# Attention loops of a four-layer model written out tile by tile, with three groups of lead, other load times, and the transposed scores first in each step

## The reference

```python
scores = jnp.einsum('bhqd,bhkd->bhqk', q, k) / np.sqrt(HEAD_DIM)   # 16 heads of 8 channels
attn = jax.nn.softmax(scores, axis=-1)
out = jnp.einsum('bhqk,bhkd->bhqd', attn, v)
```

```python
tp, ti = jax.lax.top_k(probs, TOP_K)          # TOP_K = 2 of NE = 8
def expert_step(acc, params):
    q = (x @ qw.T + qb_)...; k = (x @ kw.T + kb_)...; v = (x @ vw.T + vb_)...
    scores = jnp.einsum('bhqd,bhkd->bhqk', q, k) * scale
    p = jax.nn.softmax(scores, axis=-1)
    o = jnp.einsum('bhqk,bhkd->bhqd', p, v)
    o = o.transpose(0, 2, 1, 3).reshape(B, S, E) @ ow.T + ob_
    return (acc + o * g[..., None], None)
```

## Time and profile before

| | us |
|---|---|
| median of three runs | 4910.73 |
| the runs | 4908.14, 4910.73, 4930.10 |
| the profiled execution, its own time | 4940.64 |
| its span from first to last instruction | 4939.0 |

### The profile page before, as it was taken

The page is one execution under the profiler, slowest core; times in us unless marked ns, Lnnn a source line. Parts: engine busy times, 40 slices in busy tenths (PEclk is TensorE's granted clock), DMA queues, the critical chain, the costliest instruction groups (busy, mean ns, idle before and its releaser), DMA issues. The chain is left out here.

```text
span 4939.0 us, 142944 instructions
## 1 busy us (share of the span) xinstructions
PE 3549.6 (72%) x55309; PEld 2015.0 (41%) x55309; DVE 3202.2 (65%) x3717; ACT 2588.6 (52%) x4898; POOL 700.0 (14%) x1500
## 2 busy tenths in 40 slices
PE   1699999259998965557533288887888887888838
PEld 0355555125556732224422144444444444444414
DVE  2689889338862149984522377777777776777744
ACT  1478888127783432212111167676677666666632
POOL 0000000011000007850300011111111111111120
PEclk6799999669998977778666589898889898888868
DMA  3000000200000012200333444444444444444410
GB/s 53 18 9 8 7 8 8 38 28 13 8 5 18 17 72 86 102 18 4 37 105 109 99 91 94 94 95 89 93 92 98 86 96 87 94 89 94 94 44 21
DMA packets 173983, 286.61 MB, mean 58 GB/s; under 512 B 94796, under 2 KB 139538, under 8 KB 149134
## 3 DMA queue, kind: packets, MB, share of 16 engines
q1 hardware_dynamic: 168670, 272.05, 24.0%
q0 software_dynamic: 4656, 5.18, 0.5%
HBM read 220.57 MB, written 41.52 MB: 53 GB/s over the span
## 5 line engine op out<-in xcount | busy, mean ns | idle before, releaser
L825 ACT ACTIVATE channels_qk<-psum 128x512 f32<-128x512 f32 (+1 forms) x3908 | 2108.7, 592 | 822.6 <-PE psum L693 515.7
L887 DVE TENSOR_REDUCE l2f_chunk_max<-psum 128x2 f32<-128x1024 f32 x1168 | 1386.5, 1223 | 517.1 <-PE psum L666 510.4
L887 DVE TENSOR_REDUCE chunk_max<-psum 128x2 f32<-128x1024 f32 (+2 forms) x848 | 946.6, 1161 | 150.5 <-PE psum L666 110.6
L714 PE MATMUL psum<-channels_qk,l2f_v_and_ones 128*9 128x128 f32 x18448 | 779.7, 292 | 7.0 <-ACT channels_qk L825 5.5
L693 PE MATMUL psum<-l2f_q_parts,l2f_k_parts 51*128 51x128 bf16 x9224 | 495.5, 231 | 245.3 <-ACT channels_qk L825 116.3
L666 PE MATMUL psum<-l2f_k_parts,l2f_q_parts 48*128 48x512 bf16 x2336 | 491.1, 417 | 90.6 <-issue 69.3
L666 PE MATMUL psum<-k_parts,q_parts 48*128 48x512 bf16 (+3 forms) x1696 | 328.4, 390 | 270.4 <-DMA q_parts<-q_parts_dram 226.2
L714 PE MATMUL psum<-channels_qk,v_and_ones 128*9 128x128 f32 x12560 | 505.2, 281 | 0.1
L693 PEld LDWEIGHTS psum<-l2f_q_parts,l2f_k_parts 51*128 51x128 bf16 x9224 | 301.0, 100 | 490.8 <-ACT channels_qk L825 328.0
L714 PEld LDWEIGHTS psum<-channels_qk,l2f_v_and_ones 128*9 128x9 f32 x18448 | 417.4, 94 | 144.9 <-issue 34.2
L693 PE MATMUL psum<-q_parts,k_parts 51*128 51x128 bf16 x6280 | 324.8, 223 | 44.7 <-ACT channels_qk L825 15.1
(11 more groups left out here) (478 smaller groups left out, 3564.0 us busy)
## 6 DMA issues: line engine op xcount, KB each, us to landing
l2f_k_parts<-l2f_k_parts_dram SPq DMA_DIRECT2D x298, 192.0 KB
l2f_v_and_ones<-expert_v_dram SPq DMA_DIRECT2D x37, 1152.0 KB, 6.6
l2f_k_parts<-l2f_k_parts_dram SPq DMA_DIRECT2D x298, 128.0 KB
l2f_k_parts<-l2f_k_parts_dram SPq DMA_DIRECT2D x298, 64.0 KB
l1a_bc_rows<-ssm_rows_dram SPq DMA_DIRECT2D x16, 1024.0 KB, 5.4
expert_v_dram<-l2f_v_and_ones SPq DMA_DIRECT2D x8, 1152.0 KB
channels_qk<-ssm_rows_dram SPq DMA_DIRECT2D x8, 1024.0 KB
expert_q_dram<-heads_out SPq DMA_DIRECT2D x8, 1024.0 KB, 9.3
```

What stands on the lines that cost most here:

```text
L714: last = nc.tensor.matmul(oT[32 * m:32 * m + HD + 1, g * P:(g + 1) * P], vx(k)[:, kt, 4 * g + m, :], at.prob[:, s % 4, j, kk, pp * P:(pp + ...
L825: nc.scalar.activation(at.prob[:, s % 4, j, 0:kts, :].rearrange("p k q -> p (k q)"), c.ps[:, ring.bank(i, n), 0:kts * 2 * P], ACT.Exp, sca ...
L887: v.tensor_reduce(at.mx[:, 4 * g + 2 * pp:4 * g + 2 * pp + 2, chunk], c.ps[:, 2 * (n % 2):2 * (n % 2) + 2, 0:span.width(tile, chunk)], X, ...
```

## The change

- `each_tile` is a Python loop in all three uses. In the routed stage the first 32 tiles are straight code, and the last 8 stand in four `If(rounds > r)` of two tiles each; nothing branches back.
- The lead is 3 instead of 2 in the dense and the routed stage. The start makes three groups of first passes instead of two and sends the rows of two. In the causal stage the lead stays 4.
- Three slots for queries in all stages. The queries of tile i+2 are loaded in tile i; in the dense stage in group 0, in the routed stage at the end of group 3 (before: those of tile i+1 in group 0).
- In the routed stage SyncE loads in group 0 the keys of tile i+1, group 3, in groups 1 to 3 those of tile i+2, groups 0 to 2, and in groups 1 and 2 half the values of tile i+1 each. Before: in groups 0, 1 and 3 those of tile i+1, groups 1, 2 and 3, with group 0 of tile i+2 also in group 3, and all values in group 2. Before the first tile, three groups of keys of the second tile and its queries are loaded ahead of the first rows of a maximum.
- Side items of a routed tile: `q` after step 12 (before 21), `outT` after 14 (13), `proj` after 20 (17). POOL gathers ahead of `split_max` in group 0 and does `split_q` ahead of it in group 2.
- In each step, in all three stages, TensorE does `second_pass(s + 1)` ahead of the first pass.
- The four opening matmuls (L806), the first passes past the last tile and the second pass past the last tile of the dense stage are gone. Semaphore counts known when the code is built take the place of registers.

```diff
-        attention_loop(c, at, 2)
+        attention_loop(c, at, 3)
...
-        attention_loop(c, at, 2, routed=rt)
+        attention_loop(c, at, 3, routed=rt)
...
-        with eng.Fori(0, tiles // 2) as r:
-            with eng.If(r < rounds):
-                for k in range(2):
-                    body(r * 2 + k, k, r)
-        return rounds
+        for i in range(2 * routed.least_rounds):
+            body(i)
+        rounds = eng.value_load(routed.rounds[0:1, 0:1], min_val=routed.least_rounds, max_val=tiles // 2)
+        for r in range(routed.least_rounds, tiles // 2):
+            with eng.If(rounds > r):
+                body(2 * r)
+                body(2 * r + 1)
+        return rounds * 2
...
                 for g in range(G):
-                    load_later_max(i, g, k)
+                    load_later_max(i, g)
                     if g == 0:
-                        load_q(1 - k, i + 1)
-                        load_keys(c, at, sp, 1 - k, following, 1, k_loaded[1 - k][1])
-                    elif g == 1:
-                        load_keys(c, at, sp, 1 - k, following, 2, k_loaded[1 - k][2])
-                    elif g == 2:
+                        load_group(i + 1, 3, following)
+                    else:
+                        load_group(i + 2, g - 1, e)
+                    if g == 1 or g == 2:
                         sp.wait_ge(pv_done, span.step_base(i) + 4)
-                        load_values(1 - k, following)
-                    else:
-                        load_keys(c, at, sp, 1 - k, following, 3, k_loaded[1 - k][3])
-                        sp.wait_ge(s2_read, ring.read_when(i, ring.place(i, "proj")))
-                        store_y(i, y_stored)
-                        load_w_out(this)
-                        load_keys(c, at, sp, k, e, 0, k_loaded[k][0])
+                        load_values(i + 1, g - 1, following)
+                    if g == 3:
+                        load_q(i + 2)
+                        if i > 0:
+                            sp.wait_ge(s2_read, ring.read_when(i, ring.place(i, "proj")))
+                            sp.dma_start(routed.y_dram[i], routed.y[:, :]).then_inc(y_stored, 16)
+                            load_w_out(this)
...
                 for s in range(G * steps):
                     g, u = s // steps, s % steps
-                    group, tile, parity, load_round = first_pass_of(i, g, k, r)
+                    if s < last_step:
+                        second_pass(s + 1, i)
+                    group, tile = first_pass_of(i, g)
                     if exists(tile):
                         for unit in share(2 * span.chunks(tile), u, steps):
-                            first_pass(group, unit, tile, parity, load_round)
-                    if s < last_step:
-                        second_pass(s + 1, i, k)
+                            first_pass(group, unit, tile)
```

405 lines of the change are left out of this document (193 added, 212 removed).

## The result

| | us |
|---|---|
| changed kernel, median of four runs | 4706.6 (4688.7 to 4726.2) |
| kernel before, median of four runs | 4911.6 (4908.1 to 4930.1) |
| ratio | 0.9576, 95% interval 0.9531 to 0.9622 |
| changed kernel, profiled execution and its span | 4709.3, 4707.6 |

What follows compares the result with a forecast made beforehand. Bound: a ring of ScalarE's exponentials and TensorE's transposed scores, 1.16 us a step, plus 394 us of routed-stage stalls. Terms -212 - 182 + 3 + 22 + 12 + 6 - 38 = -389 us; forecast 4535 us, range 4480 to 4670.

Steps and rivals of the forecast that it cites:

- The bound and the undisturbed tile: Routed stage: a tile without stalls takes 41.9 us instead of 52.83; the stalls, 394 us, can be won.
- The first sub-layer: First attention stage: boundaries -42.1 us, longer start +6.1, needless opening and closing work -2; sum -38 us.
- The branch: Loop ends between pairs of tiles: writing the loop out returns 212 us in the routed stage, 42.1 in the first sub-layer.
- The rival by which only the rows' 182 us would go: Loop boundaries: their idle time has another cause than the branch and stays; -135 us, about 4790 us; chance 0.04.
- what comes next there is the steady step: Routed stage, written out: after the 18 removed boundaries of 11.8 us steps follow without new waits; -212 us.
- 0.6 us a tile for slips: Routed tiles: small timing slacks and exits of two taken conditional blocks cost +22 us, bounds 0 and 4 us per tile.
- straight code is fetched too slowly: Written-out tiles: fetching new instructions beside the loads stalls 11.8 us in each of 52 tiles; about 5150 us; chance 0.05.
- The rows and the lead: Routed stage: sending the maximum's rows 14 steps ahead instead of 6 covers both stalls of a pair; -182 us.
- The new timings that were thought tightest: Routed tiles: query loads arrive with about 2 us slack, gathered queries at 15.5 us against 17.9 needed.
- The rival of moved lateness: Routed tiles: query loads or the gather come 2 to 4 us late, +72 to +144 us; 4605 to 4680; chance 0.16.
- The order, the start and the end: Transposed scores first in each step: 0; routed stage's longer start: +12 us; jumping two conditional blocks at its end: +6.

Runs made afterwards that it cites:

- e3: The changed kernel with most of the routed stage's key and value bytes left out from tile 2 on, same number of DMAs: 4522.4 us (one run).
- e1: The kernel before with only its tiles written out; lead 2, loads and order in a step as before: 4735.9 us, ratio 0.9573.
- e7: The changed kernel with two groups of lead again in the first and the routed stage: 4740.2 us, ratio 0.9627.
- e10: e9 with the maximum's scores in front of the transposed scores again in each step: 4609.3 us, ratio 0.9339.
- e8: The kernel before, loop kept, with 64 needless small matmuls per pair of routed tiles, shifting later code blocks: 4978.0 us (one run).
- e6: The changed kernel with its routed key and value loads cut into halves and set further apart over the steps: 4600.4 us, ratio 0.9334.
- e9: The changed kernel with loads in bursts of 0.29 to 0.38 MB, keys in halves, values in quarters: 4609.0 us, ratio 0.9346.
- e11: e9 with the first routed tile's maximum rows sent ahead of the second tile's three key groups: 4598.6 us, ratio 0.9318.

## Why the prediction was wrong

**The bound and the undisturbed tile: right.** 41.9 us came from the earlier trace rows; e3 measured 41.88. That its 4522 us equal the forecast's sum on the median of before, 4522, is luck in part: it is one run, beside a kernel before of 4936.6 us, so a ratio of 0.916 where the sum has 0.921, and it does without most of the loads.

**The first sub-layer: right.** -38 forecast, -42 measured; tiles of 40.1 to 40.3 us at its start, across pairs too (49.79 before).

**The branch: right in kind.** The boundaries' time is gone with them, and e1 returned 201 us by their removal alone, of 212 + 42 forecast; in the routed stage 161 of 212, since cuts of 62 us in all took the place of part of it. The rival by which only the rows' 182 us would go (4790) fell. Of the two rules of the Trainium skill cited in the prediction, the price of a compare-and-branch in "Advanced Engine Details and Errata" is no measure of what a loop's end costs here.

**The step that failed: "what comes next there is the steady step, since the straight code inside a pair shows no such wait".** It rested on the earlier trace rows and on the loop's own passes. Both were true, and neither carries over. The causal stage has next to no loads beside it (9 GB/s from 1040 to 1480 us, against 104), and a routed pass has its block ends at the same 14 places each time. In the written-out routed stage, TensorE comes to the end of a block of 256 instructions every 6.6 us or so, at other steps in each tile, and behind a burst of loads the next block is not there. The sum held nothing for that: its only term for such losses was 0.6 us a tile for slips, with a bound of 4, and 4.8 was measured. The 4.2 us too little, in 36 tiles, are the 150 us. The range's upper end holds the bound of 4 us a tile (4535 + 122 + 8 for the start = 4665), and with 4.8 us the term alone brings 4535 to 4687, above the range. The rival "straight code is fetched too slowly" named this very mechanism, and its sign, issue waits of some us at even distances in the straight code, came true; but it was held at 0.05: I had tied it to a stall of 11.8 us a tile on the price of a boundary, and so to slower than before. At its real size, 4.2 us a tile, it costs 150 us of the forecast's 389 and stays well under the 7.5 from which it decides.

The Trainium skill says of it, in "Runtime: NRT & Kernel Launch", Instruction fetch mechanics, that the code is refilled in blocks of 16 KiB or 256 instructions, that crossing one is "mostly hidden", and that kernels prefer full unrolling where possible. The block's size is as the trace has it. That it is hidden holds in the first sub-layer and, but for one cut of 0.6 us, in e3, and not in the changed kernel's routed stage, where 61 crossings in 36 tiles cost 91 us before the clock is counted.

**The rows and the lead: right in kind, too large.** The waits are gone; but e7 puts the lead at 35 us, and e1, which keeps 83 of the 109 us of them, has the same ratio as the whole change. That a wait removed in front of another one returns only the difference fits both, and was not tested by itself: no run has the longer lead without cuts beside one that has the shorter lead without them.

**The new timings that were thought tightest** (query loads at a slack of 2 us, the gathered queries at step 12) never made TensorE wait in the routed stage; neither has a row in the wait view after the start. The rival of moved lateness gave 4605 to 4680, nearer to the result than the forecast, for a wrong reason.

**The order, the start and the end:** 0, +12 and +6 forecast; 0 (e10), +13.4 and +4.8 measured.

**What stays open.** Why the loop's passes are nearly free of cuts under the same loads. The place of the block ends has a part in it (e8); that each branch and each wait for rows lets the fetch catch up is a guess. And what the last 2 us a tile of e6, e9 and e11 are: they go with the volume (e3), not with the size of the pieces.

## What to carry to other kernels

Code written out is not free where a DMA load runs beside it: look for runs of like matmuls that are cut in two with no semaphore between, and count the instructions from cut to cut. If they are multiples of a block, spread the loads over the steps (here worth 105 us of 4705) before anything else. And a stretch that shows no wait now is evidence for its own surroundings only: ask which loads and which pauses it had, and where its blocks ended.

## What the runs showed of the hardware

Not expected, with their numbers:

- TensorE takes up 256 instructions in about 6.0 us in the first sub-layer and 6.6 in the changed kernel's routed stage (medians). From entering a block to the start of the next packet of code 3.7 us pass in the first sub-layer (median of 107) and 2.5 us in e3's routed stage, both with little data moved beside it.
- At the cuts, 2.3 to 3.9 us go by from the packet's start to the first instruction of the block. In the first sub-layer 2.2 us (median, 1.5 at least) were left from the packet's start to the block's first instruction, and TensorE did not wait.
- Behind a burst of 1.34 MB the packet started 7.7 us after the block was entered.
- After a cut of 4.09 us the granted clock was at 1.2 GHz for 6.8 us. Its mean is 0.95 in the changed kernel's routed stage, 0.99 with the loads spread (e6), 1.00 with most of them gone (e3).
